# Decoder kernel: shared products of the second 1024 rows kept as inner blocks and accumulated into the pairs' sums

## The chip, the cores and the metric

The kernel runs on one core of one Trainium2 chip. The metric is the device time of one execution in microseconds, the median of several runs. The engines are PE (matrix products), DVE and ACT (vector and activation work), POOL (here factors of norms and gathers of rows) and SP (plain DMA).

## The reference, cut to what matters

The program is a decoder of two layers over 8 x 256 tokens of 128 elements, all in f32. Each layer has attention, cross attention and a feed forward part with experts, each with a residual and a layer norm. The change lies in the first feed forward part, where each token has two of 14 routed experts and two shared ones:

```python
def _ffn(xn, rw, W1, W2):
    ms = jnp.mean(xn * xn, axis=-1, keepdims=True)
    h = xn * jax.lax.rsqrt(ms + RMS_EPS) * rw
    return jax.nn.silu(h @ W1) @ W2
...
routed_out = jnp.einsum('end,ne->nd', routed, masked)
shared = jax.vmap(lambda rw_, W1_, W2_: _ffn(xf, rw_, W1_, W2_))(rms_w_s, w1_s, w2_s).sum(0)
return (routed_out + shared).reshape(B, T, D)
...
x = _layernorm(x + _L0_ffn_ref(...), axis=-1)
x = _layernorm(x + _L1_attn_ref(...), axis=-1)
```

HID is 256, so that the inner part of a shared expert has two blocks of 128. The attention behind it (`_L1_attn_ref`) is a gated recurrence over the tokens of a batch. Its inputs are products of x with four matrices.

## The kernel before, in words

The 2048 rows are 16 tiles t of 128 tokens, or 4 chunks c of 512 (`NC_` = 4, `CH` = 512), or 8 pairs b of two tiles, a pair being one batch. The work of each engine is written out by hand in the order in which the engine does it, and engines wait for each other by counting semaphores. PSUM has 8 banks of 512 columns.

A shared product n of 16 belongs to chunk n // 4, expert n // 2 % 2 and inner block n % 2. `shared_up(n)` (L2020) is the product of a weight block with the 512 columns of XTs, into bank 4 or 5. `shared_silu(n)` (L960) has ACT apply silu and write the hidden block to slot n % 4 of `Hf`; for n of 4 and more it waits until the product that reads the slot is done (`down_done`). `shared_out(n)` (L2032) accumulates weight block x hidden block into bank c; the four of a chunk make its transposed sum. ACT copies it to `OT` (`shared_sum`, L966), PE transposes its four tiles (`shared_T`, L2038), and DVE adds them to X (`add_shared`, L1490), which counts `shared_added`.

The products of chunks 0 and 1 run before the routed experts (L2061), those of chunks 2 and 3 after them (L2119), ahead of the stage that is called the pair stage here. All routed rows have been written to memory (`yrows`) by then. POOL gathers them back in the order of the pairs, four indirect DMAs a pair, two tiles times two experts (`rows_back`, L759), into GA and GB; behind each pair's gathers stand the norm factors of the pair before (`ln_factors`, L443).

The pair stage has for each pair b: `pair_sum(b)` on PE (L2130) accumulates X and the gathered rows, weighted by the diagonal matrices `eqP`, into a PSUM bank that alternates (`sum2`); pair 0 is summed by DVE instead. DVE takes the statistics (`pair_stats`, L1521), POOL makes the factors, ACT normalises (`pair_norm`, L1008), PE transposes (`pair_T`, L2142), ACT and DVE split the result into a high and a low part (`pair_hi`, `pair_lo`). PE then has `values(b)` and two `token_products` of ten 512 column products each. ACT (`query_and_decay`, with a table change at some places) and DVE (`products_and_sums`) work on the results of each tile. PE's order in iteration b of the loop (L2183) is `token_products(2b)`, `pair_sum(b+2)`, `pair_T(b+1)`, `token_products(2b+1)`, `values(b+1)`. After the pair stage come scans over time, which DVE bounds.

Of the kernel before, what the change touches and what calls it, by code (L numbers as in the profile page):

```python
# [19 lines left out]
ACT = mybir.ActivationFunctionType  # L20
# [10 lines left out]
T = N // 128  # L31
SC = 64
CH = 512
NC_ = N // CH
# [3 lines left out]
E0, E0R, HID = 16, 14, 256  # L38
# [11 lines left out]
def decoder_program(nc, a, out):  # L50
# [53 lines left out]
    def sem(name):  # L104
        name = COUNTS_ON[name][0] if name in COUNTS_ON else name
        if name not in sems:
            sems[name] = ctx.enter_context(nc.semaphore(name))
        return sems[name]

    def on(name, n):  # L110
        return COUNTS_ON[name][1] + n
# [4 lines left out]
    with ctx:  # L116
        PS = ctx.enter_context(nc.psum_tensor("PS", [128, 8 * CH], F32))

        def bank(n, w=CH, k=1):
            return PS[:, n * CH:n * CH + (k - 1) * CH + w]  # L120
# [6 lines left out]
        ident = sb("ident", [128, 128])  # L127
# [106 lines left out]
        Hf = sb("Hf", [128, 4, CH], F32, sc)  # L234
        OT = sb("OT", [128, N], F32, sc)
        WS0 = sb("WSh", [128, E0 - E0R, 2 * HID], F32, sc)
# [220 lines left out]
        def ln_transpose(pe, n, c):  # L457
            for t in tiles(c):
                pe.wait_ge(sem("ln_x"), T * n + t + 1)
                last = pe.transpose(ln_bank(n, c)[:, t % 4 * 128:t % 4 * 128 + 128], X[:, t, :], ident[:, :])  # L460
            last.then_inc(sem("ln_T"), 1)

        def ln_bank(n, c):
            return bank(4 + c if n == 3 and c < 2 else c)
# [10 lines left out]
        def part(x, t):  # L475
            return x[:, t % 2 * 128:t % 2 * 128 + 128]

        def sum2(b):
            return bank(b % 2, S)
# [394 lines left out]
        def _(act):  # L874
# [36 lines left out]
            with act.Fori(0, B // 2) as i:  # L911
                for k in range(STEPS):
# [5 lines left out]
                    t, q4 = k % 2, k % 8 // 2  # L918
# [40 lines left out]
                scaled_T(c)  # L959
            def shared_silu(n):  # L960
                act.wait_ge(sem("up_ready"), n + 1)
                if n >= 4:
                    act.wait_ge(sem("down_done"), n - 3)
                act.activation(Hf[:, n % 4, :], bank(4 + n % 2), ACT.Silu).then_inc(sem("sg_done"), 1)

            def shared_sum(c):  # L966
                act.wait_ge(sem("down_done"), 4 * c + 4 if c >= 2 else 8)
                act.activation(OT[:, c * CH:c * CH + CH], bank(c), ACT.Copy).then_inc(sem("sums_out"), 1)

            for n in range(8):  # L970
# [28 lines left out]

            for n in range(8, 16):  # L1000
                shared_silu(n)
                if n == 14:
                    shared_sum(2)
            shared_sum(3)
            for r in range(RING):
                act.wait_ge(sem(f"ys_out{r}"), on(f"ys_out{r}", (NT - r + RING - 1) // RING * 16))

# [179 lines left out]
        def _(dve):  # L1187
# [302 lines left out]
            def add_shared(c, b):  # L1490
                dve.wait_ge(sem("sums_T"), c + 1)
                dve.wait_ge(sem("ln_x"), T + 4 * c + 4)
                x = Xp[:, S + c * CH:S + c * CH + CH]
                dve.tensor_tensor(x, x, bank(b), ALU.add).then_inc(sem("shared_added"), 1)
# [101 lines left out]
                dve.tensor_tensor(WUr[q][32:64, :, :], wu[q][:, :, :], WUr[q][0:32, :, :].bitcast(F32), ALU.subtract).then_inc(sem("wu_done"), 1)  # L1596

            pair_stats(0)
            for c in range(2, NC_):
                add_shared(c, 4 + c)  # L1600
            pair_lo(0)
            pair_stats(1)
            signed_values(0)
# [237 lines left out]
            with dve.Fori(2, E1 // 4) as i:  # L1841
                for k in range(8):
# [6 lines left out]
                    s, c = k // 4, k % 4  # L1849
# [1 line left out]
                    dve.tensor_tensor(FH[:, k % 4, :], FU[:, k % 2, :], GW[s][:, c * CH:c * CH + CH], ALU.mult).then_inc(sem("fh_done"), 1)  # L1851
            rest_f(E1 * 2, 0)
            for c in range(NC_):
                dve.wait_ge(sem("sums_T"), NC_ + c + 1)
                ln_stats(dve, 5, c, sum_bank)

        @block.tensor
        def _(pe):
# [22 lines left out]
            for n in range(2):  # L1881
                for p in range(4):
                    dst = bank(n)[:, p * 128:p * 128 + 128]
                    last = pe.matmul(dst, ctxT[:, p * 128:p * 128 + 128], wx[:, n, :], start=True, stop=True)
# [5 lines left out]
            for p in range(4):  # L1890
                last = pe.matmul(bank(2)[:, 2 * p:2 * p + 2], csq[:, p, :], halfones[:, :], start=True, stop=True)
# [47 lines left out]
            with pe.Fori(0, B // 2) as i:  # L1939
                for k in range(STEPS):  # L1940
                    g = i * STEPS + k
                    b = k // PAIRS
# [77 lines left out]
            def shared_up(n):  # L2020
                c, e, m = n // 4, n // 2 % 2, n % 2
                if n >= 2:
                    pe.wait_ge(sem("sg_done"), n - 1)
                else:
                    pe.wait_ge(sem("chosen_done"), on("chosen_done", n + 1))
                if n == 8:
                    pe.wait_ge(sem("xt_done"), on("xt_done", NT))
                    pe.wait_ge(sem("hs_done"), on("hs_done", NT))
                pe.matmul(bank(4 + m), WS0[:, e, m * 128:m * 128 + 128], XTs[:, c * CH:c * CH + CH],  # L2029
                          start=True, stop=True).then_inc(sem("up_ready"), 1)  # L2030

            def shared_out(n):  # L2032
                c, e, m = n // 4, n // 2 % 2, n % 2
                pe.wait_ge(sem("sg_done"), n + 1)
                pe.matmul(bank(c), WS0[:, e, HID + m * 128:HID + m * 128 + 128], Hf[:, n % 4, :],  # L2035
                          start=n % 4 == 0, stop=n % 4 == 3, skip_group_check=True).then_inc(sem("down_done"), 1)

            def shared_T(c, b):  # L2038
                pe.wait_ge(sem("sums_out"), c + 1)
                for t in tiles(c):  # L2040
                    last = pe.transpose(bank(b)[:, t % 4 * 128:t % 4 * 128 + 128], OT[:, t * 128:t * 128 + 128], ident[:, :])
                last.then_inc(sem("sums_T"), 1)
# [73 lines left out]
                if 2 <= i < 4:  # L2116
                    shared_T(i - 2, i - 2)

            for n in range(8, 16 + 2):  # L2119
                if n < 16:  # L2120
                    shared_up(n)
                if n >= 10:
                    shared_out(n - 2)
            pe.wait_ge(sem("ht_done"), on("ht_done", NT))
            pe.wait_ge(sem("yt_done"), on("yt_done", NT))
            for c in range(2, NC_):
                shared_T(c, 4 + c)
            pe.wait_ge(sem("l1_split"), 5)

            def pair_sum(b):  # L2130
                pe.wait_ge(sem(f"ya_in{b % 4}"), on(f"ya_in{b % 4}", b // 4 * 64 + 64))
                pe.wait_ge(sem("shared_added"), on("shared_added", b // 2 + 1))
                if b >= 3:
                    pe.wait_ge(sem("ln_x"), T * 2 + 2 * b - 2)
                pe.wait_ge(sem("diag_done"), on("diag_done", 4 * b))
                pe.matmul(sum2(b), ident[:, :], X[:, 2 * b:2 * b + 2, :].rearrange("p t d -> p (t d)"), start=True, stop=False, skip_group_check=True)
                for t in pair(b):
                    for s, y in enumerate((GA, GB)):
                        last = pe.matmul(part(sum2(b), t), eqP[:, s, t, :], y[:, t, :], start=False, stop=s == 1, skip_group_check=True)
                last.then_inc(sem("y_sum"), 1)  # L2140

            def pair_T(b):  # L2142
# [28 lines left out]

            pair_T(0)
            pair_sum(1)
            pe.wait_ge(sem("shared_added"), on("shared_added", NC_))
            pe.wait_ge(sem("ln_lo"), NC_ + 1)
            token_products(0)
            values(0)
# [289 lines left out]
            for k in range(3):  # L2467
                f_down(E1 * 2 + k, k)
            for t in range(T):
                pe.wait_ge(sem("sums_out"), NC_ + t // 4 + 1)  # L2470
                last = pe.transpose(bank(4 + t // 4)[:, t % 4 * 128:t % 4 * 128 + 128], OT1[:, t * 128:t * 128 + 128], ident[:, :])
                if t % 4 == 3:
                    last.then_inc(sem("sums_T"), 1)
# [41 lines left out]
```

## Time and profile before

| what | value |
|---|---|
| median of 3 runs | 1024.8 us (1024.53 to 1025.45) |
| the profiled execution | 1031.13 us, span 1029.4 us |
| PE busy over the span | 941.8 us (91%) |
| DVE busy | 779.1 us (76%) |
| ACT busy | 578.6 us (56%) |
| POOL busy | 422.7 us (41%) |
| mean granted TensorE clock | 0.963 |

The shares are means over stages with different limits; what a stage is bound by is read from the rows of that stage. Times in rows are microseconds from the start of the span. "issue" is time in which an engine waited for nothing that the profile shows. A full f32 product is recorded as two matmuls, so that "x2" is one product of 512 columns. The ends of matmuls are modelled.

### The profile page before, as it was taken

What the parts mean: (1) busy time and instruction counts of PE and PEld (TensorE: products, weight loads), DVE (VectorE), ACT (ScalarE), POOL (GpSimd) and SP (SyncE); (2) the same over time, 40 slices, a digit from 0 to 9 for tenths busy, and PEclk for the clock granted to TensorE, in tenths of its full rate; (3) what the DMA queues carried; (4) which work ended last, traced back from release to release, by engine and by line L of the source; (5) the groups of instructions that cost most, each with busy time, mean ns of one, the idle gap of its engine ahead of it and who ended that gap; (6) DMA issues with size and microseconds to landing.
All of it is one profiled execution on the core that took longest, in us unless ns stands there. A gap on an engine that the chain in (4) does not pass through costs nothing.

```text
span 1029.4 us, 18171 instructions
## 1 busy us (share of the span) xinstructions
PE 941.8 (91%) x5491; PEld 784.8 (76%) x5491; DVE 779.1 (76%) x2040; ACT 578.6 (56%) x1360; POOL 422.7 (41%) x487
## 2 busy tenths in 40 slices
PE   6999999999998898999887789988979999999994
PEld 6899999999996555775666677876657888888883
DVE  4766766766666983652799899967679999999995
ACT  3666666666666644443686333516655555655655
POOL 4565656566565315544550767633650000000001
PEclk8999999999998978999998899999989999999998
DMA  7232223223223202341101222001016666666651
GB/s 259 68 117 85 92 90 100 98 84 108 88 94 112 98 22 59 84 77 44 32 21 43 83 82 83 1 1 62 0 34 173 183 178 176 183 176 168 175 146 41
DMA packets 46980, 98.31 MB, mean 96 GB/s; under 512 B 7106, under 2 KB 23170, under 8 KB 45779
## 3 DMA queue, kind: packets, MB, share of 16 engines
q1 hardware_dynamic: 44466, 92.64, 29.4%
q0 software_dynamic: 2464, 5.05, 2.5%
q8 instruction: 26, 0.43, 0.2%
q14 instruction: 24, 0.19, 0.1%
HBM read 75.25 MB, written 22.41 MB: 95 GB/s over the span
## 4 chain that ended last, share of the span: by engine, by line
PE 38%; issue 20%; POOL 18%; DVE 14%; ACT 5%; DMA 2%; SPq 1%; POOLq 0%; another core or an unknown queue 0%; DVEq 0%; ACTq 0%
PE PS L1860 8%; PE PS L1861 8%; PE PS L1862 8%; POOL P L678 7%; POOL WS L687 3%; PE PS L2086 3%; POOL WS L683 3%; PE PS L2100 2%; DVE rb L1658 2%; ACT Xp L454 2%; DVE keep L1644 2%; PE PS L2029 1%; PE PS L2035 1%; DMA rw<-in_rw 1%; POOL WS L701 1%
## 5 line engine op out<-in xcount | busy, mean ns | idle before, releaser
L678 POOL TENSOR_TENSOR P<-P,rl 128x256 f32<-128x256 f32 (+1 forms) x130 | 104.9, 828 | 118.9 <-DVE rl L1259 118.9
L447 POOL TENSOR_TENSOR rs<-ms,neghalf 128x4 f32<-128x4 f32 (+1 forms) x28 | 26.0, 929 | 279.6 <-DVE nm L441 279.5
L1252 DVE CUSTOM_DVE_ANT_0 P<-PS,cmask 128x128 f32<-128x128 f32 (+1 forms) x260 | 77.1, 352 | 69.7 <-issue 69.6
L1177 ACT ACTIVATE FG<-PS 128x512 f32<-128x512 f32 x112 | 67.1, 599 | 92.6 <-PE PS L1862 92.6
L907 ACT ACTIVATE P<-P,mn 128x128 f32<-128x128 f32 (+1 forms) x260 | 114.3, 443 | 1.9 <-DVE mn L1252 1.9
L1860 PE MATMUL PS<-XTh,W 128*128 128x512 f32 x256 | 100.5, 393 | 1.2 <-DMA W<-w3s 0.2
L1931 PE MATMUL PS<-VO,PT 128*128 128x128 f32 x804 | 100.6, 275 | 0.0
L1861 PE MATMUL PS<-XTl,W 128*128 128x512 f32 x256 | 99.7, 390 | 0.0
L1862 PE MATMUL PS<-XTh,W 128*128 128x512 f32 x256 | 99.7, 389 | 0.0
L1931 PEld LDWEIGHTS PS<-VO,PT 128*128 128x128 f32 x804 | 95.0, 192 | 0.0
L1846 DVE TENSOR_TENSOR FU<-FG,PS 128x512 f32<-128x512 f32 x112 | 77.1, 688 | 17.1 <-ACT FG L1177 3.1
L1829 DVE TENSOR_TENSOR FHL<-FH,FHH 128x512 fp32r<-128x512 f32 x128 | 89.1, 696 | 0.9 <-ACT FHH L1163 0.9
L1163 ACT ACTIVATE FHH<-FH 128x512 fp32r<-128x512 f32 x128 | 80.9, 632 | 8.4 <-DVE FH L1838 6.7
L915 ACT ACTIVATE Uh<-PS 128x512 fp32r<-128x512 f32 x64 | 38.4, 599 | 71.2 <-PE PS L1862 71.2
L1264 DVE COPY PT<-PS 128x768 f32<-128x768 f32 x66 | 62.5, 947 | 2.9 <-PE PS L1920 2.9
L756 POOL DMA_INDIRECT XG<-xrows,tok x45 | 42.8, 952 | 50.4 <-DVE tok L1483 20.7
L1860 PEld LDWEIGHTS PS<-XTh,W 128*128 128x128 f32 x256 | 48.0, 188 | 15.8 <-issue 5.6
L1920 PE MATMUL PS<-ident,P 128*128 128x128 f32 x396 | 56.8, 280 | 2.1 <-POOL P L678 2.1
L1862 PEld LDWEIGHTS PS<-XTh,W 128*128 128x128 f32 x256 | 48.0, 188 | 10.1
L1861 PEld LDWEIGHTS PS<-XTl,W 128*128 128x128 f32 x256 | 48.1, 188 | 9.2
L919 ACT ACTIVATE VO<-PS 128x512 f32<-128x512 f32 x64 | 38.4, 601 | 27.6 <-PE PS L1862 27.6
L1860 PE MATMUL PS<-FHH,W 128*128 128x512 f32 x128 | 50.6, 396 | 1.8 <-DVE FHL L1829 1.7
(476 smaller groups left out, 2613.8 us busy)
## 6 DMA issues: line engine op xcount, KB each, us to landing
GI<-coef SPq DMA_DIRECT2D x56, 256.0 KB, 4.2
GW<-coef SPq DMA_DIRECT2D x56, 256.0 KB, 4.1
w3s<-WS SPq DMA_DIRECT2D x32, 384.0 KB, 2.6
W<-w3s SPq DMA_DIRECT2D x32, 384.0 KB, 3.3
Wb<-decay SPq DMA_DIRECT2D x7, 1024.0 KB, 4.6
WR<-in_w SPq DMA_DIRECT2D x32, 192.0 KB, 2.4
WR<-in_w SPq DMA_DIRECT2D x16, 256.0 KB, 2.8
w12f<-WS SPq DMA_DIRECT2D x16, 256.0 KB, 2.1
```

The lines of the kernel that those rows point to most:

```text
L678: last = pool.tensor_tensor(v, v, f, ALU.mult)
L907: last = act.activation(P[:, slot, c:c + w], P[:, slot, c:c + w], ACT.Exp, scale=-1.0, bias=mn[:, par, q:q + 1], accum_out=ls[:, par, q:q ...
L1163: act.activation(FHH[:, (k - 1) % 4, :], FH[:, (k - 1) % 4, :], ACT.Copy).then_inc(sem("fhh_done"), 1)
L1177: act.activation(FG[:, k % 2, :], bank(4 + k % 2), ACT.Silu).then_inc(sem("fg_done"), 1)
L1252: dve.tensor_tensor_reduce(out=P[:, slot, c:c + w], in0=scores(par, q), in1=cmask[:, 256 - w:256], scale=1.0, scalar=3e38, op0=ALU.add, op ...
L1264: dve.tensor_copy(PT[:, k % 2, :, :], PTP).then_inc(sem("pt_done"), 1)
L1829: dve.tensor_tensor(FHL[:, (k - 1) % 4, :], FH[:, (k - 1) % 4, :], FHH[:, (k - 1) % 4, :].bitcast(F32), ALU.subtract).then_inc(sem("fhl_do ...
L1846: dve.tensor_tensor(FU[:, k % 2, :], FG[:, k % 2, :], bank(6 + k % 2), ALU.mult).then_inc(sem("ft_done"), 1)
L1860: pe.matmul(dst, l[0], r[0], start=start, stop=False, skip_group_check=skip)
L1861: pe.matmul(dst, l[0], r[1], start=False, stop=False, skip_group_check=skip)
L1862: return pe.matmul(dst, l[1], r[0], start=False, stop=stop, skip_group_check=skip)
L1931: last = pe.matmul(OB[:, dst:dst + 128], PT[:, par, h, blk * 128:blk * 128 + 128], VO[:, half, 2 * p + h, :], start=first, stop=(p == PAIR ...
```

## The change

The output products of chunks 2 and 3 (n = 8 to 15) aren't made ahead of the pair stage. Their hidden blocks stay in SBUF: n = 8 to 11 in `Hf`, n = 12 to 15 in `OT`, which is free by then. Each `pair_sum(b)` with b of 4 and more accumulates, for each of its two tiles, four products (hidden block of the tile as the stationary operand, 128 columns of the weights as the moving one), eight in all, directly into the pair's sum by row. The copies, transposes and adds of chunks 2 and 3 go away. PE has 16 products of the identity with itself between the last hidden block and the pair stage. The counts of `sums_out` and `sums_T` that are used again at the end of the kernel fall by 2.

```diff
+        def hidden_rows(n):
+            return OT[:, n % 4 * CH:n % 4 * CH + CH] if n >= 12 else Hf[:, n % 4, :]
+
@@ ACT
             def shared_silu(n):
                 act.wait_ge(sem("up_ready"), n + 1)
-                if n >= 4:
+                if 4 <= n < 12:
                     act.wait_ge(sem("down_done"), n - 3)
-                act.activation(Hf[:, n % 4, :], bank(4 + n % 2), ACT.Silu).then_inc(sem("sg_done"), 1)
+                elif n >= 12:
+                    act.wait_ge(sem("sums_T"), 2)
+                act.activation(hidden_rows(n), bank(4 + n % 2), ACT.Silu).then_inc(sem("sg_done"), 1)
 
             def shared_sum(c):
-                act.wait_ge(sem("down_done"), 4 * c + 4 if c >= 2 else 8)
+                act.wait_ge(sem("down_done"), 8)
...
             for n in range(8, 16):
                 shared_silu(n)
-                if n == 14:
-                    shared_sum(2)
-            shared_sum(3)
@@ DVE
             pair_stats(0)
-            for c in range(2, NC_):
-                add_shared(c, 4 + c)
             pair_lo(0)
@@ PE
-            for n in range(8, 16 + 2):
-                if n < 16:
-                    shared_up(n)
-                if n >= 10:
-                    shared_out(n - 2)
+            for n in range(8, 16):
+                shared_up(n)
+            pe.wait_ge(sem("sg_done"), 16)
             pe.wait_ge(sem("ht_done"), on("ht_done", NT))
             pe.wait_ge(sem("yt_done"), on("yt_done", NT))
-            for c in range(2, NC_):
-                shared_T(c, 4 + c)
+            for _ in range(16):
+                pe.matmul(bank(6)[:, 0:128], ident[:, :], ident[:, :], start=True, stop=True)
             pe.wait_ge(sem("l1_split"), 5)
 
             def pair_sum(b):
                 pe.wait_ge(sem(f"ya_in{b % 4}"), on(f"ya_in{b % 4}", b // 4 * 64 + 64))
-                pe.wait_ge(sem("shared_added"), on("shared_added", b // 2 + 1))
+                if b < 4:
+                    pe.wait_ge(sem("shared_added"), on("shared_added", b // 2 + 1))
+                else:
+                    pe.wait_ge(sem("ln_x"), T * 2)
...
                         last = pe.matmul(part(sum2(b), t), eqP[:, s, t, :], y[:, t, :], start=False, stop=s == 1, skip_group_check=True)
+                    if b >= 4:
+                        for n in range(t // 4 * 4, t // 4 * 4 + 4):
+                            e, m = n // 2 % 2, n % 2
+                            last = pe.matmul(part(sum2(b), t), hidden_rows(n)[:, t % 4 * 128:t % 4 * 128 + 128],
+                                             WS0[:, e, HID + m * 128:HID + m * 128 + 128], start=False, stop=n % 4 == 3, skip_group_check=True)
...
             pair_sum(1)
-            pe.wait_ge(sem("shared_added"), on("shared_added", NC_))
             pe.wait_ge(sem("ln_lo"), NC_ + 1)
```

## Rows read from the trace of the kernel before

**Rows 1.** Busy time by stretch: width, PE, PEld, DVE, ACT, POOL, clock, DMA
```profile
468.00:482.00 14.00, 14.00 (x36) 6.12 (x35) 2.49 (x12) 5.55 (x10) 8.78 (x11) 1.00 0.18 47
503.90:510.90 7.00, 6.75 (x38) 5.65 (x37) 6.21 (x15) 5.27 (x11) 3.48 (x5) 1.00 0.10 26
```
**Rows 2.** Chain of waits: start, us, what
```profile
516.73 0.89 PE PS L2139 x8
```
**Rows 3.** Instructions of PE, 468 to 500 us: start, us, what, idle before
```profile
479.33 2.74 PE L2035 MATMUL PS<-Hf,WSh 128*128 128x512 f32 x6
481.90 0.60 PE L2041 MATMUL PS<-ident,OT 128*128 128x128 f32 x4
482.75 0.66 PE L2041 MATMUL PS<-ident,OT 128*128 128x128 f32 x4 [0.25 <-ACT OT L968]
483.61 0.41 PE L2147 MATMUL PS<-ident,Xp 128*128 128x128 f32 x2 [0.20 <-ACT Xp L1011]
484.95 0.39 PE L2139 MATMUL PS<-GB,keep 128*128 128x128 f32 x2
486.26 0.47 PE L2162 MATMUL PS<-abr,onesr 128*128 128x512 f32 x1 [0.92 <-DVE Xp L1494]
489.49 0.70 PE L2136 MATMUL PS<-Xp,ident 128*128 128x256 f32 x2 [0.32 <-DMA GB<-yrows,pidx]
492.43 0.19 PEld L1860 LDWEIGHTS PS<-wdh,XTh 128*128 128x128 f32 x1 [0.46 <-ACT QS L1027]
498.24 0.39 PE L1860 MATMUL PS<-XTh,wdh 128*128 128x256 f32 x1 [4.16 <-DVE XTl L1543]
```
**Rows 4.** Instructions of POOL, ACT and DVE in the same stretch
```profile
480.54 0.75 POOL L447 TENSOR_TENSOR rs<-ms,neghalf 128x2 f32<-128x2 f32 x1
482.10 0.60 ACT L968 ACTIVATE OT<-PS 128x512 f32<-128x512 f32 x1 [1.98 <-issue]
482.60 0.86 ACT L1011 ACTIVATE Xp<-Xp,nb,rs 128x128 f32<-128x128 f32 x2
485.09 0.69 DVE L1494 TENSOR_TENSOR Xp<-Xp,PS 128x512 f32<-128x512 f32 x1 [1.46 <-remote]
488.00 0.49 DVE L1533 BATCH_NORM_STATS2 st<-PS 128x6 f32<-128x128 f32 x2 [1.89 <-remote]
489.07 0.73 POOL L447 TENSOR_TENSOR rs<-ms,neghalf 128x2 f32<-128x2 f32 x1 [2.40 <-DVE nm L441]
490.11 0.81 ACT L1011 ACTIVATE Xp<-PS,nb,rs 128x128 f32<-128x128 f32 x2 [4.60 <-POOL nb L449]
```
**Rows 5.** Instructions in order of time, 515 to 525 us
```profile
516.38 0.64 ACT L1029 ACTIVATE ZA<-ZA 128x512 f32<-128x512 f32 x1
517.35 0.68 DVE L1554 TENSOR_REDUCE PROD<-ZA 128x16 f32<-128x512 f32 x1
517.87 0.41 PE L2147 MATMUL PS<-ident,Xp 128*128 128x128 f32 x2 [0.25 <-issue]
524.85 0.41 PE L2147 MATMUL PS<-ident,Xp 128*128 128x128 f32 x2 [0.25 <-issue]
```
**Rows 6.** Instructions of DVE and PE, 530 to 534 us
```profile
530.75 0.69 DVE L1554 TENSOR_REDUCE PROD<-ZA 128x16 f32<-128x512 f32 x1 [1.36 <-ACT ZA L1029]
533.44 0.61 PE L2169 MATMUL PS<-ident,ABs 128*32 128x128 f32 x4 [1.64 <-ACT Xp L1011]
```
**Rows 7.** Identity products in order of time; a line's instructions, ns min/median/max
```profile
350.27 3.29 PE L2012 MATMUL PS<-ident 128*128 128x128 f32 x28
L2139 PEld LDWEIGHTS PS<-GA,keep x28: 188/191/192, 484.1 to 531.2; 128*128 128x128 f32 x28
```
**Rows 8.** An idle time of PE, and stretches at a lower granted clock
```profile
389.23 1.39 PE L2035 MATMUL PS<-Hf,WSh 128*128 128x512 f32 x2 [2.40 <-ACT Hf L964]
389.96:396.79 6.83, 5.90 (x18) 3.76 (x17) 1.30 (x4) 1.85 (x4) 3.77 (x4) 0.50 0.19 46
499.19:502.60 3.41, 3.41 (x10) 2.64 (x9) 2.97 (x5) 2.18 (x5) 2.80 (x3) 0.50 0.14 38
```

## What I expected of the change, and why

> **What bounds the kernel now.** I read three views in this order. First the busy time by stretch, to see which stages the change touches. In 468 to 482 us the shared products fill PE from end to end, while ACT is busy for 5.6 of 14 us. In the pair stage behind it nothing has much room: from 503.9 to 510.9 us, one pair, PE is busy 6.75 of 7.00 us and DVE 6.21 [rows 1]. Busy shares can't say which of the two sets the pace, so the chain of waits comes second: there the piece around 516 us is PE work, among it the four gather products of a pair sum at 0.89 us [rows 2]. Third come the rows of single instructions, to see who waits ahead of each step. PE waits 0.25 us ahead of `pair_T`, and DVE starts a product of signs at 517.35, 0.33 us after the sigmoid that it needs ended at 517.02 [rows 5]. So between 503 and 525 us PE sets the pace, ACT follows within 0.25 us, DVE within 0.33 us. From 530.75 us on the bound is another: DVE stood 1.36 us for ACT, and PE stood 1.64 us for ACT at 533.44 [rows 6], since ACT loads two tables there; behind that DVE works off its scans.
>
> **Part 1, ahead of the pair stage.** Removed on PE: eight products of 512 columns. Three of them run from 479.33 to 481.90, 0.857 us each [rows 3], so 6.86 us; and eight transposes, four of which take 0.45 us at their pitch, so 0.9 us and a wait for ACT. Removed on ACT and DVE: two copies of 0.60 us and two adds of 0.69 us [rows 4]. Added on PE: 16 identity products. The 14 that stand elsewhere (28 records) fill 3.29 us [rows 7], so 16 fill about 3.6 us. The eight `shared_up` products stay, 0.857 us each from 468.1 on, so they end near 475.0; the last silu, as long as such a copy, ends at 475.7; the identity products end near 479.4. PE is 3 to 4 us early. That buys almost nothing, because of what is late next: `pair_T(0)` needs the norm of pair 0, its factors come from POOL, and POOL starts them at 480.54 behind the eight gathers of its queue [rows 4]. They end at 481.57. Now ACT's norm starts at 482.60 because the copy of the sums stands ahead of it; without the copy it starts at 481.6. So `pair_T(0)` moves from 483.61 to 482.6, 1.0 us, with PE idle for 3 us ahead of it.
>
> **Part 2, the first two pairs.** `token_products(0)` stands at 486.26 behind the second add of DVE [rows 3, 4]; without it, about 484.4. This gain is lost at once: `pair_sum(2)` waits for gathered rows until 489.49 [rows 3], and POOL's issue of them doesn't move. What does pass on is the sum of pair 1. `pair_sum(1)` ends at 485.34 by its record, yet DVE reads the sum at 488.00 [rows 3, 4]: 2.64 us late, a delay of the signal that the trace doesn't explain (the transposes that end at 483.41 release DVE only at 485.09). POOL is free of its gathers and two memsets at 486.67 and idles until 489.07, when the statistics are there; ACT's norm of pair 1 follows at 490.11 [rows 4]. In the changed kernel `pair_sum(1)` ends near 484.35. With a prompt signal the factors start at 486.7 and the norm near 487.65, 2.45 us earlier; with the same 2.64 us of delay the sum is seen at 487.0, 1.0 us earlier. ACT, DVE and POOL then carry this gain through the first two tokens to `values(1)` at 498.24, ahead of which PE stands for 4.16 us [rows 3]. I take the middle, 1.7 us. The lower bound is 0 (the signal comes at a fixed time).
>
> **Part 3, the clock.** Behind those 4.16 us of standing the granted clock is 0.50, the 1.2 GHz level, from 499.19 to 502.60 us, with PE busy all of it; the same follows the idle 2.40 us at 389.23 [rows 8], and none follows the 1.64 us at 533.44 [rows 6]. At the full level that work would take 1.7 us less, of which ACT's steps for the next token, as long as now, leave about 1.4. In the changed kernel the standing is 4.16 + 0.46 (a wait of PE for ACT that falls away [rows 3]) less the gain of part 2: 2.9 us with 1.7, over the 2.40 that were enough, so I keep the slow stretch and give this term 0. With 2.45 us of gain it is 2.2 us, and the 1.4 us may be saved. The new idle 3 us ahead of `pair_T(0)` may bring a slow stretch too; the 3.4 us of work behind it would take up to 1.7 us more, which the wait until 489.49 covers.
>
> **Part 4, the products in the pair sums.** Each of `pair_sum(4)` to `pair_sum(7)` gets eight products of 128 x 128. They have the shape of the gather products, four of which take 0.89 us [rows 2], so eight take 1.78 us. As columns that is no loss: 0.2225 us for 128 columns stands against 0.857 us for 512. But it is moved from a stretch where PE had time to one where it has none. In iterations 2, 3 and 4, PE has 0.25 us ahead of `pair_T` [rows 5] and nothing else, so each adds 1.78 - 0.25 = 1.53 us, three add 4.6 us. `pair_sum(7)` lies ahead of the 1.64 us that PE stands for ACT [rows 6]; it adds 0.14 us there, which DVE's work covers. If that cover were gone it would cost 1.5 us. The lateness reaches the end: `pair_T(5)` releases ACT's split, two table loads and the next sigmoid, which DVE waits for at 530.75 [rows 6], and DVE then has its scans and no idle time to the stage's end. Each new wait at the head of these sums (`ln_x` at 32) has long been met; nothing is queued behind it.
>
> A rule of the Trainium skill speaks against this part. Its page "TensorE: Matmul & The Clock Gate", section "Back-to-back issue gap", has a stream of load and product at 81 ns for 128 columns and 131 ns for 512, so that narrow products cost about 2.5 times as much a column. By that estimate eight products take 4.2 us and not 1.78, and the sum would be about 1035. The rows above are for this shape and type, and I go by them.
>
> **Sum.** +4.6 (part 4) - 1.7 (part 2) - 0 (part 3) = +2.9 us. In the profiled execution, 1031.13 us with a span of 1029.4, that is 1034.0; against the median of the runs, 1024.8, it is 1027.7. The two differ by 6.3 us, and I take the difference to be the same for both kernels. About 2 us, 0.2%, is what a measurement can tell.
>
> **Rivals.**
> Everything at the front comes through: the signal is prompt (-2.45) and the clock holds (-1.4). Then +4.6 - 3.85 = +0.75, 1025.6 us. With the prompt signal alone it is +2.15, 1026.9. For it: 2.2 us of standing lies under 2.40. Against: both are needed, and in the unprofiled runs the delay may be missing before the change too, which leaves little to gain (POOL free at 486.67 against statistics at 487.1, some 0.5 us). Chance of the first 0.2.
>
> Nothing comes through: the sum of pair 1 is seen at 488 as now. +4.6, 1029.4 us. Chance 0.12.
>
> The other side: DVE sets the pace of the pair stage and the products hide. DVE is busy 6.21 us of 7.00 [rows 1] and little less than PE. Then the front's 2.45 us stay, 1022.4 us. It decides when DVE lags its inputs by over 1.53 us a pair; the rows have 0.33 [rows 5]. Chance 0.12.
>
> The narrow products don't overlap their loads. A load of this shape is busy 191 ns [rows 7]; laid ahead of each of the 16 records at 0.11 us instead of under the one before, eight products take 4.8 us, three pairs add 13.7 us, and the sum is +12, 1036.8 us. The gather products at 0.89 us for four contradict it, since they have the same loads. The page named above leans to this side. Chance 0.03.
>
> **How the numbers follow.** Forecast (1026.5 to 1028.9) 0.53, and 0.2, 0.12, 0.12, 0.03 for the others. The range that leaves no more than 2 in 10 out reaches from the first rival, 1025.6 with a little below it for a slow stretch less elsewhere, to the second: 1025.0 to 1029.6. The faster side, 0.12, stays outside. Slower by over 2.05 us: most of the forecast, the second and the last, 0.63. Same: the first rival and the forecast's low edge, 0.25. Faster 0.12.
>
> **What would show it.** In the changed kernel: identity products ending near 479.4, PE idle 3 us, `pair_T(0)` near 482.6; the first wait for gathered rows still ends near 489.5; the norm of pair 1 between 487.6 and 489.1; `pair_sum(4)` to `(6)` at 3.1 us instead of 1.3, with 8.5 us from one `pair_T` to the next where 7.0 are now (517.87 to 524.85 [rows 5]) and no wait ahead of them; DVE with about 1 us of idle time in each of these pairs; `pair_T(5)` near 527.8 where it is 524.85, and all that follows the pair stage 2.9 us later than now. The forecast is wrong if the pairs still follow each other at 7 us, if a product of the new kind takes other than 0.22 us, or if `values(1)` moves by more than 2.5 us.

## Result and profile after

The changed kernel is slower. In the comparison that was made first it takes 1030.4 us (median of 12 runs, 1025.1 to 1031.8) against 1024.7 for the kernel before (12 runs, 1019.1 to 1027.8); the ratio of the runs is 1.0046, 95% interval 1.0031 to 1.0061, so +4.7 us with 3.2 to 6.3 (the medians alone differ by 5.7). Forecast were +2.9.

| what | before | after |
|---|---|---|
| profiled execution, span | 1031.13, 1029.4 us | 1025.22, 1023.5 us |
| PE busy | 941.8 us | 938.9 us |
| DVE, ACT, POOL busy | 779.1, 578.6, 422.7 us | 777.4, 578.3, 422.6 us |
| mean granted TensorE clock | 0.963 | 0.966 |
| `shared_up(8)` to the first state scan | 90.64 us | 91.10 us |

The profiled execution of before (1031.13) is slower than all twelve of its runs, and that of after (1025.22) is the second fastest of its twelve. Comparing the two as they stand gives a gain that no comparison of times shows; most of this text is about that.

The stretches that answer to [rows 1] and [rows 8]: the one ahead of the pair stage, one pair, and a stretch at the lower clock. Columns are width, busy time (and instructions) of PE, PEld, DVE, ACT and POOL, granted clock, DMA share, GB/s.

```profile
460.30:474.30 14.00, 11.18 (x50) 6.02 (x48) 2.49 (x12) 5.43 (x10) 8.84 (x11) 1.00 0.18 48
509.26:517.58 8.32, 8.32 (x53) 7.39 (x52) 6.93 (x16) 5.27 (x11) 4.78 (x6) 1.00 0.13 34
476.21:479.62 3.41, 3.41 (x12) 2.83 (x11) 1.03 (x7) 0.00 (x0) 2.77 (x6) 0.50 0.20 50
```

A pair takes 8.32 us instead of 7.00, and PE has no idle time left in it. The instructions of PE, which answer to [rows 3, 5, 6] (start, us, what, idle time before and what ended it):

```profile
468.32 3.84 PE L2125 MATMUL PS<-ident 128*128 128x128 f32 x32 [0.69 <-ACT OT L969]
474.95 0.41 PE L2153 MATMUL PS<-ident,Xp 128*128 128x128 f32 x2 [2.79 <-ACT Xp L1013]
...
488.02 0.39 PE L1860 MATMUL PS<-XTh,wdh 128*128 128x256 f32 x1 [3.23 <-DVE XTl L1545]
...
514.48 0.59 PE L2137 MATMUL PS<-Xp,ident 128*128 128x256 f32 x2
514.90 0.38 PE L2140 MATMUL PS<-GA,keep 128*128 128x128 f32 x2
515.12 0.39 PE L2140 MATMUL PS<-GB,keep 128*128 128x128 f32 x2
515.35 1.06 PE L2144 MATMUL PS<-WSh,OT 128*128 128x128 f32 x8
516.24 0.39 PE L2140 MATMUL PS<-GA,keep 128*128 128x128 f32 x2
516.47 0.39 PE L2140 MATMUL PS<-GB,keep 128*128 128x128 f32 x2
516.69 1.06 PE L2144 MATMUL PS<-WSh,OT 128*128 128x128 f32 x8
517.58 0.38 PE L2153 MATMUL PS<-ident,Xp 128*128 128x128 f32 x2
...
533.55 0.41 PE L2153 MATMUL PS<-ident,Xp 128*128 128x128 f32 x2 [1.57 <-ACT Xp L1013]
```

Read the starts, not the durations: four new products (x8 records) run from 515.35 to 516.24, 0.89 us; the whole sum takes 3.10 us, and `pair_T` follows at once. The identity products end at 472.16, PE stands 2.79 us ahead of `pair_T(0)`, and 3.23 us ahead of `values(1)`. POOL, ACT and DVE at the front, which answer to [rows 4], and DVE in a pair:

```profile
478.75 0.12 POOL L775 MEMSET mb<- 32x1 f32 x1
478.79 0.12 POOL L776 MEMSET db<- 32x1 f32 x1
478.84 0.75 POOL L447 TENSOR_TENSOR rs<-ms,neghalf 128x2 f32<-128x2 f32 x1
```
```profile
477.05 0.50 DVE L1535 BATCH_NORM_STATS2 st<-PS 128x6 f32<-128x128 f32 x2 [0.81 <-PE PS L2140]
...
512.36 0.42 DVE L1549 TENSOR_SCALAR VS<-PS 128x256 f32<-128x256 f32 x1 [0.95 <-PE PS L1862]
```

Here DVE reads the sum of pair 1 without the delay of [rows 4], and now has idle time of 0.95 us in a pair. The statistics of pair 1 are there at 478.09, yet POOL begins the factors at 478.84, straight behind its gathers and two memsets.

### The profile page after: what moved, and what is told of

It reads as the page before. It is cut to its first block, busy times and chain, and to the rows that moved or that the text cites. A ratio compares the mean times of both kernels' runs of the same rounds, so it can differ in the third digit from the quotient of the medians.

```text
span 1023.5 us, 18308 instructions
## 1 busy us (share of the span) xinstructions
PE 938.9 (92%) x5563; PEld 786.7 (77%) x5563; DVE 777.4 (76%) x2038; ACT 578.3 (57%) x1358; POOL 422.6 (41%) x487
## 4 chain that ended last, share of the span: by engine, by line
PE 38%; issue 20%; POOL 20%; DVE 14%; ACT 4%; DMA 2%; SPq 1%; POOLq 0%; DVEq 0%; ACTq 0%
PE PS L1860 8%; PE PS L1861 8%; PE PS L1862 8%; POOL P L681 8%; POOL WS L690 3%; PE PS L2086 3%; POOL WS L686 3%; DVE rb L1658 2%; PE PS L2100 2%; DVE keep L1644 2%; ACT Xp L454 1%; DMA rw<-in_rw 1%; DVE PS L1632 1%; POOL WS L704 1%; POOL gb L800 1%
## 5 line engine op out<-in xcount | busy, mean ns | idle before, releaser
L1179 ACT ACTIVATE FG<-PS 128x512 f32<-128x512 f32 x112 | 67.2, 600 | 92.5 <-PE PS L1862 92.5
```

The lines of the kernel that those rows point to most:

```text
L1179: act.activation(FG[:, k % 2, :], bank(4 + k % 2), ACT.Silu).then_inc(sem("fg_done"), 1)
```

## Experiments

To compare traces, times are counted from `shared_up(8)`, the first product of the changed part; "the stage" is from there to the first state scan. Each row of the table is one trace. "Late" marks those in which signals of PE reach ACT or DVE 0.9 us or more behind the end of the matrix product (2 to 7 cases in each); the other eight traces, called prompt, have not one. The comparisons were made on several chips of the same kind; late traces came from those on which the kernel before has medians of 1031.0 and 1032.0 us (and the first profile, at 1031.13, is such a trace), the others from those on which it has 1024.5 to 1024.7. Ratios are those of the runs, each with its own runs of the kernel before beside it.

| kernel | signals | norm of pair 1 | `pair_T(2)` | `pair_T(2)` to `(5)` | first state scan | ratio to before (95%) |
|---|---|---|---|---|---|---|
| before, first profile | late | 22.04 | 35.83 | 20.95 | 90.64 | |
| before, again | prompt | 19.55 | 33.34 | 20.93 | 88.10 | 1.0015 (0.9994 to 1.0036) |
| after, first profile | prompt | 19.59 | 32.24 | 25.03 | 91.10 | 1.0046 (1.0031 to 1.0061) |
| after, again | prompt | 19.57 | 33.37 | 25.02 | 92.21 | 1.0075 (1.0051 to 1.0098) |
| after, third time | prompt | 19.99 | 33.91 | 25.04 | 92.77 | 1.005 (1.0028 to 1.0071) |
| no products in the sums | prompt | 19.81 | 33.60 | 20.97 | 88.42 | 1.0017 (0.9997 to 1.0036) |
| by row, ahead of the stage | prompt | 19.58 | 33.50 | 20.99 | 88.34 | 1.003 (1.0016 to 1.0044) |
| the same and a fill | prompt | 19.55 | 32.19 | 21.04 | 87.06 | 1.0001 (0.998 to 1.0022) |
| no identity products | prompt | 19.92 | 33.72 | 25.03 | 92.55 | 1.0094 (1.0064 to 1.0125) |
| table early | late | 22.03 | 34.50 | 20.97 | 89.31 | 0.9978 (0.9962 to 0.9994) |
| table early and fill | late | 22.08 | 33.31 | 21.02 | 88.18 | 0.9966 (0.9951 to 0.9981) |
| products doubled | late | 21.99 | 36.37 | 30.39 | 100.57 | 1.0059 (1.0039 to 1.0079) |
| after, table early and fill | late | 22.01 | 33.71 | 25.04 | 93.53 | 1.0025 (1.0005 to 1.0045) |
| after, last gather behind | late | 21.12 | 33.75 | 25.03 | 93.25 | 1.0023 (1.0007 to 1.0039) |

### Both kernels again

The changed kernel with no edit:

> The changed kernel once more, to see where its time lies against the profile of it that I have. Theory A (the products cost, the front gives some back): the pair stage alone moves, by +0.5 to +4.6 us, and the rows of the 45 expert slots are as long as before the change, so that the ratio is 1.0005 to 1.0045. Theory B (most of the lateness lies outside the pair stage): the ratio is 1.003 to 1.006 again, and a trace of an execution near 1030 us has the pair stage as in the one at 1025 us, but some 5 us more between the first and the last of the 45 slots.

It took 1031.9 us against 1024.5. A third comparison, on another chip, with the kernel before against itself beside it:

> The changed kernel a third time, for a third trace. From the second count, 1.003 to 1.008. Theory B: from the first shared product of row 1024 to the first state scan 91 to 92.5 us, 2 to 3.5 us over the kernel before in its own undisturbed trace; what is left of the ratio must then stand in other stages, and the slots are the first place to look (67 to 73 us).

> The kernel before against itself: ratio 1.000 within 0.002, and a second trace of it. Theory A: the 45 slots take 73 us as in the first trace, and the sum of pair 1 is seen by DVE over 2 us after its record's end, as there. Theory B (the execution that I read was burdened by late signals of PE, which is 5 us over the median): the slots take 67 to 69 us here, the sum of pair 1 is seen within 0.1 us, the norm of pair 1 then comes 1 to 2 us earlier, and the pair stage up to the first state scan takes 89 us and not 90.6.

They took 1029.6 and 1025.9 against 1024.5. The traces that are free of late signals are the ones to subtract; of the kernel before there is only one, and it is the fastest of its ten runs (1021.2 us). Front of the kernel before, again (POOL's last gathers of pair 2, then the factors; DVE; ACT; PE):

```profile
478.54 0.94 POOL L762 DMA_INDIRECT GB<-yrows,pidx  x1 [0.30 <-issue]
479.48 0.11 POOL L772 MEMSET mb<- 32x1 f32 x1
479.52 0.11 POOL L773 MEMSET db<- 32x1 f32 x1
479.57 0.74 POOL L447 TENSOR_TENSOR rs<-ms,neghalf 128x2 f32<-128x2 f32 x1
```
```profile
478.49 0.49 DVE L1533 BATCH_NORM_STATS2 st<-PS 128x6 f32<-128x128 f32 x2 [0.59 <-PE PS L2139]
```
```profile
480.62 0.81 ACT L1011 ACTIVATE Xp<-PS,nb,rs 128x128 f32<-128x128 f32 x2 [3.18 <-POOL nb L449]
...
482.90 1.28 ACT L1029 ACT_TABLE_LOAD   x1
```
```profile
488.74 0.39 PE L1860 MATMUL PS<-XTh,wdh 128*128 128x256 f32 x1 [3.52 <-DVE XTl L1543]
```

`shared_up(8)` stands at 461.07 here. DVE reads the sum 17.42 behind it (19.93 in the first profile), and POOL is free of its queue at 18.50 and starts the factors in that moment; the norm follows at 19.55. In the first profile after the change these are 16.74, 18.53 and 19.59: the sum is 0.7 us earlier and the norm is not. POOL's queue of gathers, which the change doesn't touch, ends 18.5 us behind `shared_up(8)` in every trace but the last. The two kernels below with the products ahead of the stage say the same: their sum is read at 17.00, and the factors start at 18.49 and 18.52.

In the other two traces after the change it is not POOL that takes the gain. The slow stretch behind the idle time ahead of `pair_T(0)` falls on `pair_sum(1)` itself. The second trace, PE and DVE:

```profile
479.12 0.64 PE L2140 MATMUL PS<-GA,keep 128*128 128x128 f32 x2
479.55 0.64 PE L2140 MATMUL PS<-GB,keep 128*128 128x128 f32 x2
```
```profile
481.07 0.49 DVE L1535 BATCH_NORM_STATS2 st<-PS 128x6 f32<-128x128 f32 x2 [1.54 <-PE PS L2140]
```

Each product of the sum takes 0.43 us there instead of 0.22. DVE reads the sum 17.44 us behind `shared_up(8)`, as late as before the change (17.42), and in the third trace 17.88, so that the factors start at 18.52 and 18.94. `values(1)` stands at 27.67 before and at 27.71, 27.70 and 28.11 after. The three traces after the change differ among themselves by the clock:

```profile
478.79:482.21 3.42, 3.30 (x13) 3.15 (x14) 0.47 (x2) 0.38 (x1) 2.51 (x4) 0.50 0.17 43
...
492.45:495.86 3.41, 3.41 (x10) 2.83 (x11) 2.27 (x5) 0.70 (x2) 2.55 (x5) 0.50 0.07 19
```

These are stretches of the third: one behind the 2.77 us that PE stands ahead of `pair_T(0)`, one behind `values(1)` as in both traces of before. Only the first profile after the change lacks the second of them, and by it `pair_T(2)` is 1.1 us earlier. Against the kernel before with prompt signals, the stage is 4.1 us longer (second trace of after) and 4.7 (third); in the first, without that slow stretch, it is 3.0.

### What the products cost

The changed kernel without its 32 products in the sums (`if b >= 4:` and its loop are deleted):

> The changed kernel without the 32 products in the pair sums, so the shared part of the second 1024 rows is left out. Theory A: the pair sums return to 1.3 us, the three PE-bound iterations lose 1.53 us each, and it is 4.6 us faster than the changed kernel, 1.5 to 3.5 us faster than the kernel before (ratio 0.9965 to 0.9985). Rival (DVE bounds the pair stage): it is as fast as the changed kernel within 1 us. Theory B: it stays slower than the kernel before or at it, by what the stage outside costs.

1025.35 against 1024.5 us. The pitch is back at 6.99 us, the stage at 88.42:

```profile
504.94:511.93 6.99, 6.74 (x36) 5.59 (x36) 6.71 (x16) 5.27 (x11) 4.55 (x6) 1.00 0.15 40
```

So the three pairs cost 4.1 us in the traces. In the times the products cost 1.0017 against the mean of the three comparisons of the changed kernel, 1.0057: 4.1 us again, though with some 2 us of uncertainty (against the changed kernel of the same comparison, at 1.0075, it is 5.9). The freed front brings no gain: 88.42 stands against 88.10 of before. The other way to the same price, eight more products in each of the three sums:

```diff
-                        for n in range(t // 4 * 4, t // 4 * 4 + 4):
+                        for n in list(range(t // 4 * 4, t // 4 * 4 + 4)) * (2 if b < 7 else 1):
```

> The changed kernel with the shared products of pair_sum(4), (5) and (6) made twice, 16 instead of 8 each; the shared part of pairs 4 to 6 then stands twice in the output. If PE sets the pace of those iterations and the price is the products' own time, each pair takes 8 x 0.2225 = 1.78 us more, 8.35 + 1.78 = 10.1 us from one pair_T to the next in three iterations, +5.3 us in all against the changed kernel (1029.6 to 1030.4 by its runs), about 1035.3. If part of the first 1.78 us had been hidden by DVE or the like, the second step would cost visibly more than the first (first: 1.35 us a pair in the traces). If narrow products lost time to their loads in some other way, the pitch of a product would differ from 0.2225 us.

```profile
513.70:523.80 10.10, 10.10 (x69) 9.17 (x68) 6.95 (x15) 5.26 (x11) 4.77 (x6) 1.00 0.10 26
```

6.98, 8.35, 10.13 us a pair for 0, 8 and 16 products. The second step is 1.78 us, just 8 x 0.2225; of the first, 0.42 us was hidden. The whole cost 6.1 us by its runs (4.0 to 8.2) where the traces of the late kind differ by 9.2 from end to end; it had only 5 runs, and the gap is not explained. Nor is the changed kernel itself on record with late signals, so that by the times the second step can't be told.

### The products ahead of the stage

The kernel before with the by-row products from kept blocks, but ahead of `pair_sum(1)` into banks 2 and 3, with DVE's two adds kept and no identity products:

```diff
-            for c in range(2, NC_):
-                shared_T(c, 4 + c)
+            for t in range(8, T):
+                c = t // 4
+                for n in range(4 * c, 4 * c + 4):
+                    e, m = n // 2 % 2, n % 2
+                    last = pe.matmul(bank(c)[:, t % 4 * 128:t % 4 * 128 + 128], hidden_rows(n)[:, t % 4 * 128:t % 4 * 128 + 128],
+                                     WS0[:, e, HID + m * 128:HID + m * 128 + 128], start=t % 4 == 0 and n % 4 == 0, stop=n % 4 == 3, skip_group_check=True)
```

> The kernel before with the sums made by row from the kept blocks, but ahead of the pair stage: 32 products of 128 x 128 into banks 2 and 3 right after the last silu, in place of the 16 identity products, then two adds by DVE; nothing in the pair sums. The products take 7.1 us from 475.7, so they end at 482.8, when the norm of pair 0 is due. Theory A: the front's gain without the price, pair_T(0) 0.8 us earlier and the norm of pair 1 by up to 2.4 us, ratio 0.9965 to 0.9990. Theory B: slower than the kernel before, as the changed one is, by 2 us or more.

1027.7 us. The stage takes 88.34 us, 3.9 us less than in the second trace of the changed kernel, which has the same slow stretch behind `values(1)`: the place is the price, not the shape. `pair_T(0)` stands 15.3 behind `shared_up(8)` instead of 15.5. The time is nonetheless above that of before by 1.6 to 4.5 us, and the stage has only 0.2 of it; 0.4 us appear in the scans and 1.4 in the first round of the attention loop, whose code is the same (below).

The same with 12 identity products ahead of `values(1)`:

> The kernel with the products by row ahead of the pair stage, and 12 identity products more ahead of values(1), where PE stands for 3 to 4 us. If the slow stretch of the clock behind this idle time costs what I put for it, 1.4 us, this is 1.0 to 1.4 us faster than the same kernel without them and pair_T(2) follows pair_T(1) after 10.5 us instead of 12.0; if the stretch is hidden, no difference.

```profile
489.63 2.84 PE L2188 MATMUL PS<-ident 128*128 128x128 f32 x24
493.29 0.39 PE L1862 MATMUL PS<-XTh,wdh 128*128 128x256 f32 x1 [0.82 <-DVE XTl L1545]
```

PE stands 0.82 us instead of 3.49, no slow stretch follows, and the stage is 1.28 us shorter (87.06). That is the price of the slow stretch behind `values(1)`; 1.4 had been estimated.

### Without the identity products

The changed kernel without its 16 identity products, which leave nothing to the output:

> The changed kernel without the 16 identity products, so that PE stands from 475.7 to 482.6 us of the old time scale. Theory A: the slow stretch of the clock that follows doubles the work behind it at most until the gathered rows come; within 1 us of the changed kernel. Rival (the clock at the front is what costs): a slower pair_sum(1) delays the norm of pair 1, 1 to 2.5 us slower than the changed kernel.

1033.3 us, 1.4 us above the changed kernel of the same comparison (1031.9); the ratios, 1.0094 and 1.0075, have intervals that overlap. Its stage is not longer (92.55 us); 1.2 us are in the attention loop. So the identity products neither help nor harm the stage: PE stands 7.29 us instead of 2.8 ahead of `pair_T(0)`, a longer slow stretch follows (6.83 us, from 476.75), and yet `pair_T(0)` is as early and the norm of pair 1 is at 19.92, as in the third trace of after. With 5 runs the rest can't be told from nothing.

### A table earlier, and a fill

The trace of before, again, shows what does set `values(1)`: ACT, which stands 3.18 us for the factors of pair 1 and then loads a table for 1.28 us. Two additions to the kernel before:

```diff
             pair_norm(0)
             pair_hi(0)
+            act.activation(QS[:, 1, 0:1], ident[:, 0:1], ACT.Sigmoid)
             pair_norm(1)
...
             token_products(1)
+            for _ in range(8):
+                pe.matmul(bank(1)[:, 256:384], ident[:, :], ident[:, :], start=True, stop=True)
             values(1)
```

> The kernel before, with two additions ahead of values(1): one sigmoid of 128 x 1 on ACT ahead of pair_norm(1), so that the table of the sigmoid is loaded in ACT's idle time (in the second trace of before ACT stands 3.18 us for the factors of pair 1, from 477.43 to 480.62, and loads the table for 1.28 us at 482.90, on the way to DVE's first products), and 8 identity products on PE ahead of values(1), 1.8 us of the 3.52 us that PE stands there. If ACT's table load sets values(1) and the idle time of PE brings the slow stretch behind it, as the traces of before and of rows_ahead with fill say, the first falls by 1.28 us and the second by 1.3: up(8) to state scan 0 falls from 88.1 (undisturbed before) to 85.5 us and the time to about 1022, ratio 0.9975. Rival: the front is held by POOL's queue alone or by DVE, the table load is covered and only the clock counts: 86.8 us in the pair stage, 1023.3. Rival: POOL's gathers of pair 2 hold pair_sum(2), and nothing of the table's 1.28 us comes through but the clock is kept.

> The kernel before with the early sigmoid on ACT alone, no identity products. If ACT's table load is on the path, PE's idle time ahead of values(1) falls from 3.52 to 2.24 us and values(1) stands 1.28 us earlier behind up(8), 26.4 us instead of 27.7. The clock: idle times of 2.40 us and more were followed by a slow stretch in before, one of 2.11 to 2.74 us sometimes in the others, so either the slow stretch stays (pair stage 86.8 us, 1023.3) or it goes (85.5 us, 1022). If the table load is covered, 88.1 us and 1024.6.

```profile
485.23 0.38 ACT L1015 ACTIVATE XTh<-PS 128x256 fp32r<-128x256 f32 x1 [2.36 <-remote]
485.63 1.28 ACT L1055 ACT_TABLE_LOAD   x1
486.93 0.20 ACT L1055 ACTIVATE QS<-ident 128x1 f32<-128x1 f32 x1
489.55 0.81 ACT L1011 ACTIVATE Xp<-PS,nb,rs 128x128 f32<-128x128 f32 x2 [2.42 <-POOL nb L449]
```

This is the kernel with both: the table is loaded while ACT would stand for POOL anyway. The traces are late ones, and so is the first profile of before, to which they are compared: the stage falls from 90.64 to 89.31 with the table, to 88.18 with the fill too. Both came out near the forecast (1.28 and 1.3), with 1.33 and 1.13 us. The times are 0.9978 and 0.9966 of before, -2.3 and -3.5 us; by its ratio the version with both is the fastest kernel measured here, and faster than both kernels of this case. (The stage has 2.5 us of the 3.5.) The sigmoid starts 1.30 us behind the start of its table load. The Trainium skill, page "ScalarE: Activation LUTs", section "What ACT_TABLE_LOAD costs", adds a drain of 1.38 us to a load of 1.28. As an estimate from these figures, the move would have been worth 2.66 us; the trace does not agree in this place, where the load takes 1.28 us and 1.33 were gained.

The same two additions to the changed kernel:

> The changed kernel with the same two additions as the kernel of the table and the fill: early sigmoid on ACT and 8 identity products ahead of values(1). With both fronts freed of the table load and of the slow stretch, what the change costs should be the products alone, 3 x 1.35 = 4.1 us, plus up to 0.5 us from the slow stretch that the idle time of PE ahead of pair_T(0) brings: pair stage 89.6 to 90.2 us against 85.5 of before with the same additions, and about 1026.5 against 1022. If the change had a hidden gain at the front that only the table load covered (pair_T(0) stands 0.9 us earlier), the difference would be 3.2 us or less.

1.0025 against 0.9966: 6.1 us between the two kernels, with some 2.5 of uncertainty. In the stage it is 5.35: 4.02 from the products, 0.40 at the front, and 0.93 behind `pair_T(5)`, whose signal came 0.96 us late in this trace. A hidden gain at the front isn't there.

### The last gather behind the factors

The changed kernel, in which POOL issues the fourth gather of pair 2 behind the factors of pair 1:

> The changed kernel with the fourth gather of pair 2 issued by POOL behind the factors of pair 1 instead of ahead of them. Two modes have been seen in the traces. With prompt signals, the norm of pair 1 starts 19.55 us behind up(8) before the change and 19.59 after it, because POOL comes free of its gathers at 18.45 in both, although in the changed kernel the statistics are there at 17.8. If POOL's queue is what takes the front's gain, the factors now start near 17.9 and the norm near 18.9, and values(1) stands near 27.0 instead of 27.7; pair_sum(2) waits up to 1.2 us longer for its rows, which PE's 3.2 us of standing ahead of values(1) cover; in all 0 to 0.7 us faster than the changed kernel, too little for its runs to tell, so that the trace decides. With late signals, the statistics are seen 19.9 us behind up(8) in both kernels; then the norm of pair 1 stays near 22.0, unless the lateness is tied to POOL's gathers, in which case the signal comes 1.25 us earlier, at the new end of the queue.

```profile
481.20 0.94 POOL L767 DMA_INDIRECT GB<-yrows,pidx  x1 [0.30 <-issue]
482.14 0.11 POOL L777 MEMSET mb<- 32x1 f32 x1
482.17 0.11 POOL L778 MEMSET db<- 32x1 f32 x1
485.04 0.73 POOL L447 TENSOR_TENSOR rs<-ms,neghalf 128x2 f32<-128x2 f32 x1 [2.76 <-DVE nm L441]
```
```profile
483.64 0.42 DVE L1549 TENSOR_TENSOR XTl<-PS,XTh 128x256 fp32r<-128x256 f32 x1 [7.30 <-ACT XTh L1021]
483.98 0.48 DVE L1539 BATCH_NORM_STATS2 st<-PS 128x6 f32<-128x128 f32 x2
```

The trace is a late one, so that the case with prompt signals wasn't seen; that POOL's queue holds the norm there rests on the rows, not on this run. But it says something of the lateness. In all five late traces with the old order DVE sees the sum of pair 1 at 19.88 to 19.97 us behind `shared_up(8)`, before the change and after it, 1.5 us behind the end of POOL's fourth gather, though PE ends the sum anywhere from 16.4 to 17.8. With that gather moved away DVE reads it at 19.02, straight behind its step before. So the delay of this signal doesn't go with when PE ends, and the run speaks for the gathers. It doesn't show them to be the cause: ACT, which stands for the signal of `pair_T(0)` in the row below, sees it at 18.26 here, and at 18.36 and 18.41 in the two late traces after the change with the old order.

```profile
483.22 0.38 ACT L1021 ACTIVATE XTh<-PS 128x256 fp32r<-128x256 f32 x1 [3.79 <-remote]
```

## Why the forecast was right and where it failed

The direction was right, and +4.7 us lies nearer to a rival than to the forecast. The ratio puts the time at 1029.5 on the base of 1024.8, the range ended at 1029.6; the median of that comparison, 1030.4, is above it, and so are the ratios of the other two (1.005 and 1.0075, 1029.9 and 1032.5 on the same base). That the time lies inside the range, by 0.1 us, is luck in part: the range reached just to the rival without any gain at the front, 1029.4 us, and the 0.6 to 1.2 us in the scans, which no sum had, were offset in part by 0.5 us too much for the products.

**Part 1 held.** Counted from `shared_up(8)`, identity products were to end at 11.3 and ended at 11.85; `pair_T(0)` was to come at 14.5 and came at 14.64, with 2.79 us of standing for 3. The slow stretch that was thought possible behind it came in all three traces after the change. The wait for gathered rows was to cover it; but `pair_sum(1)` lies ahead of that wait, and the stretch doubled it in two of the three.

**Part 2 failed: 1.7 us were booked, 0 came.** The rows were read rightly and did not stand for the kernel. The delay of 2.64 us in [rows 4] was what the gain rested on; it belongs to the late kind of execution, and the median, as far as the traces tell, was taken from the prompt kind. With prompt signals the sum of pair 1 comes 0.7 us earlier in one trace after the change, but POOL's gathers end at the time at which the old sum was ready anyway; in the other two the slow stretch keeps the sum from coming earlier at all. The norm is at 19.55 before and at 19.57 to 19.99 after. With late signals the sum is seen at 19.9 in both kernels. The forecast had named the prompt case ("leaves little to gain") without a chance of its own, and had the late one as the rival in which nothing comes through, with 0.12. It is this rival's size, +4.6 and 1029.4 us, that came true; its mechanism is that of the late traces, and the prompt ones have another. What should have raised it: [rows 4] has POOL free of its queue at 486.67, only 0.4 us ahead of the 487.1 at which statistics with a prompt signal were ready, so that a prompt signal leaves at most that.

**Part 3 held in size, not in its reasoning.** The term was 0, and the slow stretch behind `values(1)` is there in two of three traces after the change and in both of before. It costs 1.28 us (kernel with the fill). But a length of standing doesn't decide it: 3.23 us brought none in the first profile of after, 3.20 us did in the second. One more place was not foreseen, behind the pair stage. The second diff of the first scans (trace of before, again, then third trace of after):

```profile
555.94 1.98 PE L2234 MATMUL PS<-keep,less_half 128*128 128x512 f32 x4 [0.55 <-DVE keep L1644]
```
```profile
563.83 3.53 PE L2239 MATMUL PS<-keep,less_half 128*128 128x512 f32 x4 [2.11 <-DVE keep L1644]
```

PE fills its time ahead of it with a fixed number of identity products. When a slow stretch fell into them, as before the change, they lasted to 0.55 us ahead of the second diff; in two of three traces after the change (the first and the third) they ran at full clock, were done 2.11 us early, and the slow stretch fell on the four products of the second diff, which DVE waits for. From the first state scan to the last it takes 97.6 us in both traces of before and 98.8, 98.2 and 98.8 after; the 0.6 us of the second trace stand at later products. This is +0.6 to +1.2 us that the sum lacked. The kernel without the products has 97.6 as well and the doubled one too, while kernels with the old pair sums have up to 99.9 (the one with products by row and a fill). So it seems to depend on where the work comes to lie against the clock's changes, not on the edit as such; no run was made to show it.

**Part 4 held, and was 0.5 us too dear.** 0.89 us for four products, 3.10 for a sum, DVE with 0.95 us of idle time, `pair_sum(7)` for nothing (from `pair_T(5)` to the first state scan 33.83 us before and after): all as said. A pair costs 1.36 instead of 1.53. The 0.25 us of idle time in [rows 5] are counted from the modelled end of the record before; by the starts, the last gather product stands at 517.23 and `pair_T` at 517.87, 0.64 us apart where 0.22 are usual. 0.42 us were free. Three pairs make 4.1, not 4.6. The eight narrow products also answer the Trainium skill, page "TensorE: Matmul & The Clock Gate", section "Back-to-back issue gap": the ratio of 2.5 that the forecast worked out from its two figures doesn't hold for this type, in which 0.2225 us for 128 columns stand against 0.857 us for 512.

**The base.** "The difference is the same for both kernels" (6.3 us from profile to median) was wrong: for the changed kernel it is 5.1 us the other way. The sum with what the runs showed is 4.1 for the products, 0 for the front, 0 to 0.5 for the stretch behind `pair_T(0)`, and 0.6 to 1.2 in the scans: 4.7 to 5.8 us, where the three comparisons have 4.7, 7.7 and 5.1; the second, 5.2 to 10.0 by its interval, is met only at its lower end. From `shared_up(8)` to the end the traces take 558.4 us before (the prompt one) and 563.2, 563.4 and 565.1 after, 4.8 to 6.8 more. The rest of the distance between traces lies ahead of the changed code: `shared_up(8)` stands at 461.07 before and at 460.31, 463.63 and 464.29 after.

## What to carry over

Before a delay in a profile is booked as a gain, ask whether the profiled execution is of the kind that the median is made of: here it was 6.3 us slower, and a second trace of the same kernel would have shown that the delay was not there. Then look who else holds the step that is to come earlier: a queue that ends at the same time takes the gain, or a slow stretch behind idle time that the change itself brings. And work that is moved from an engine's idle time into a stage which that engine sets is paid, less the little that the engine has free there (1.36 of 1.78 us a pair here). Read free time of PE from the distance of starts, not from the end of a record.

## What the runs showed of the hardware

Signals of PE were late by 1 to 3.4 us in six of 14 traces, each time while POOL issued indirect gathers or at most 1.7 us behind one. The medians of the kernel before are 6.3 to 7.5 us higher on the chips of five of the six. Its two traces are 10 us apart, and 5.6 of them lie in the 45 expert slots, where POOL gathers too: 73.0 us from the first slot to the last with late signals, 67.4 without. (Over all kernels it is 70.6 to 73.9 and 67.2 to 70.0.) That the gathers cause it is not shown, and why some chips or executions have it stays open.

The first round of the attention loop takes 1.2 to 1.4 us more in four of the kernels (by row ahead, the same and a fill, no identity products, after with table and fill) and in no trace of the others, of which before has two and after three. Up to the last exponential of the loop these four need 293.0 to 293.2 us and the others 291.5 to 291.8. The code of that loop is the same in all. This points to the program and not to the execution, though each of the four has only one trace; what about it was not settled, and it clouds every comparison here that is finer than 1.4 us, that of the products ahead of the stage above all.
